# The adapter's first three effective matrices, made during the seventh pair of routed experts

## The reference

```python
# third layer, for each expert e
h = jax.nn.gelu(context_c @ ew1[e] + eb1[e], approximate=True)
y = h @ ew2[e] + eb2[e]
out = out + w_be[:, e][:, None, None] * mask[e][None, :, None] * y
...
# fourth layer: a1, b1, a2, b2 are (B, D, 8), made from the conditioning alone
u = jnp.einsum('btd,bdr->btr', x, a2)
mid = jnp.einsum('btd,dl->btl', x, base_down) + jnp.einsum('btr,blr->btl', u, b2)
mid = jax.nn.gelu(mid, approximate=False)
v = jnp.einsum('blr,btl->btr', b1, mid)
out = jnp.einsum('btl,kl->btk', mid, base_up) + jnp.einsum('bkr,btr->btk', a1, v)
return x + out
```

## Time and profile before

| | us |
|---|---|
| median of 3 runs | 1182.06 (1181.74 to 1182.39) |
| the profiled execution's own time | 1186.63 |
| its span, first to last instruction | 1184.8 |
| PE busy | 1136.6 |
| DVE busy | 766.9 |
| ACT busy | 608.0 |
| POOL busy | 364.4 |
| mean granted PE clock | 0.960 |

### The profile page before, as it was taken

The page is one execution under the profiler, slowest core; times in us unless marked ns, Lnnn a source line. Parts: engine busy times, 40 slices in busy tenths (PEclk is TensorE's granted clock), DMA queues, the critical chain, the costliest instruction groups (busy, mean ns, idle before and its releaser), DMA issues. The chain is left out here.

```text
span 1184.8 us, 58156 instructions
## 1 busy us (share of the span) xinstructions
PE 1136.6 (96%) x23706; PEld 1014.0 (86%) x23706; DVE 766.9 (65%) x2954; ACT 608.0 (51%) x2147; POOL 364.4 (31%) x1372
## 2 busy tenths in 40 slices
PE   5899999999999999999999999899999999999898
PEld 4788888888889888999999998678888888888687
DVE  6566666666666666565565657687666666666697
ACT  4456566566566565555565554533333333333476
POOL 3654344344434344444444440063000000000121
PEclk7759999989989999999999999899999999999899
DMA  8211202202102011110000000000000000000022
GB/s 243 74 44 39 79 4 80 79 4 79 53 31 79 29 54 26 14 15 12 5 4 4 5 4 4 3 1 2 2 2 2 2 1 2 2 2 2 5 75 86
DMA packets 44432, 37.14 MB, mean 31 GB/s; under 512 B 24280, under 2 KB 39946, under 8 KB 44172
## 3 DMA queue, kind: packets, MB, share of 16 engines
q1 hardware_dynamic: 43564, 33.12, 9.2%
q10 hardware_dynamic: 608, 0.30, 0.1%
HBM read 28.42 MB, written 4.98 MB: 28 GB/s over the span
## 5 line engine op out<-in xcount | busy, mean ns | idle before, releaser
L1268 PEld LDWEIGHTS bank<-LH,seq 128*128 128x128 f16 x8192 | 248.8, 96 | 54.0 <-DVE LH L842 46.5
L1268 PE MATMUL bank<-LH,seq 128*128 128x16 f16 x8192 | 283.1, 170 | 12.3 <-DVE LH L842 10.3
L568 ACT ACTIVATE gel<-bank,seq 128x256 f32<-128x256 f32 x256 | 121.5, 475 | 215.0 <-PE bank L1173 211.3
L1171 PE MATMUL bank<-XHL,WE 128*128 128x256 f16 x768 | 210.6, 274 | 5.7 <-issue 2.9
L1171 PE MATMUL bank<-GH,WE 128*128 128x256 f16 x768 | 210.6, 274 | 2.2 <-DVE GH L815 1.8
L1172 PE MATMUL bank<-XHL,WE 128*128 128x256 f16 x768 | 210.7, 274 | 0.0
L1173 PE MATMUL bank<-XHL,WE 128*128 128x256 f16 x768 | 210.7, 274 | 0.0
L1172 PE MATMUL bank<-GH,WE 128*128 128x256 f16 x768 | 210.7, 274 | 0.0
L1173 PE MATMUL bank<-GH,WE 128*128 128x256 f16 x768 | 210.6, 274 | 0.0
L1274 PE MATMUL bank<-LH,seq 128*128 128x16 f16 x4096 | 177.2, 169 | 2.3 <-issue 2.3
L399 POOL TENSOR_TENSOR RH<-rf,RH 128x32 f16<-128x32 f32 x256 | 64.6, 252 | 355.9 <-ACT RH L525 355.9
(11 more groups left out here) (193 smaller groups left out, 2539.6 us busy)
## 6 DMA issues: line engine op xcount, KB each, us to landing
stage<-in_L_cond_ew SPq DMA_DIRECT2D x8, 1024.0 KB, 8.6
stage<-in_L_cond_W SPq DMA_DIRECT2D x8, 1024.0 KB, 5.4
XHL<-in_x SPq DMA_DIRECT2D x8, 512.0 KB, 9.0
out<-WE SPq DMA_DIRECT2D x16, 256.0 KB, 2.1
stage<-in_L_cond_sw SPq DMA_DIRECT2D x2, 1024.0 KB, 5.5
scratch<-rows SPq DMA_DIRECT2D x96, 8.0 KB, 2.3
stage<-in_L_cond_Wx SPq DMA_DIRECT2D x1, 1024.0 KB, 9.1
stage<-in_L_cond_Wh SPq DMA_DIRECT2D x1, 1024.0 KB, 11.3
```

The costliest lines, as they stand in the source:

```text
L568: nc.scalar.activation(gel[:, m % 2, :], banks[m % len(banks)][:, 0:256], ACT.Gelu_apprx_tanh, scale=scale, bias=bias).then_inc(s["a_g"], 1)
L1171: MM(out_, w(HI), x(HI), start=start, stop=False, skip_group_check=True)
L1268: MM(z, LW[:, h, 1, c, tile * P:(tile + 1) * P], LH[:, old, HI, c], start=False, stop=False, skip_group_check=True)
```

## The change

The three matrices (0, 0), (0, 1) and (1, 0) are made during the seventh pair (i = `EARLY_PAIR` = 6). PE calls `matrix` ahead of the slots n = 4, 12 and 20. DVE calls `add_eff` after the split of tile n = 8, 16 and 24 and `weff_lo` after that of n = 14, 22 and 30 (`early_matrix`). ACT calls `weff_hi` after the gelu of n = 12, 20 and 28. For this the three get a home in `seq`, the buffer in which the recurrent layers' weights stood, behind X3; the fourth home of `weff` stays in `WE`. The float32 sum of all three goes through `early_f`, the unused last quarter of a staging buffer. The calls ahead of step 0 fall away. Step 1 on PE gets a wait for the last routed sums (`v_x3`), because mid(1) writes the banks 6 and 7.

```diff
-        weff = adead[:, 0:4096].rearrange("p (s q h c n) -> p s q h c n", s=2, q=2, h=2, c=C)
+        beside = 2 * place[0] + 4096
+        assert beside + 3072 <= 12288
+        weff_home = {(0, 0): seq[:, beside:beside + 1024], (1, 0): seq[:, beside + 1024:beside + 2048],
+                     (0, 1): seq[:, beside + 2048:beside + 3072], (1, 1): adead[:, 0:1024]}
+        weff = {at: home.rearrange("p (h c n) -> p h c n", h=2, c=C) for at, home in weff_home.items()}
+        early_f = dead[:, 3 * C * D:4 * C * D].rearrange("p (c n) -> p c n", c=C)
+        EARLY = ((0, 0), (0, 1), (1, 0))
+        EARLY_PAIR = B // 2 - 2
...
# ACT, in routed_pair after the gelu of slot n
+                    if i == EARLY_PAIR and n in (12, 20, 28):
+                        e = EARLY[n // 8 - 1]
+                        weff_hi(*e, e[1], True)
...
# ACT, ahead of adapter_steps
-            for n, b in ((0, 0), (0, 1), (1, 0)):
-                weff_hi(n, b, b, True)
...
# DVE
+            def early_matrix(n):
+                k, stage_ = divmod(n - 8, 8)
+                if stage_ == 0:
+                    dve.wait_ge(s["v_ad"], 2)
+                    if k:
+                        dve.wait_ge(s["v_w0"], k)
+                    add_eff(*EARLY[k], EARLY[k][1], True)
+                elif stage_ == 6:
+                    weff_lo(*EARLY[k], EARLY[k][1])
...
# DVE, in routed_pair after routed_split(i, n)
+                    if i == EARLY_PAIR and 8 <= n < 32:
+                        early_matrix(n)
...
# DVE, ahead of adapter_steps
-            for n, b in ((0, 0), (0, 1), (1, 0)):
-                add_eff(n, b, b, True)
-            for n, b in ((0, 0), (0, 1), (1, 0)):
-                weff_lo(n, b, b)
...
# PE, in routed_pair ahead of the products of slot n
+                    if i == EARLY_PAIR and n % 8 == 4 and n < 24:
+                        if n == 20:
+                            pe.wait_ge(s["v_ad"], 1)
+                        matrix(*EARLY[n // 8], EARLY[n // 8][1], n != 12)
...
# PE, in step
+                    if b == 1:
+                        pe.wait_ge(s["v_x3"], 6 + 6 * B)
...
# PE, ahead of adapter_steps
-            matrix(0, 0, 0, True)
-            matrix(0, 1, 1, False)
-            matrix(1, 0, 0, True)
```

More of the change, by code:

```diff
@@ L644, in x3_hi, with weff_hi @@
                                      ACT.Copy).then_inc(s["a_x3"], 1)
+            def weff_hi(n, b, slot, first):
+                act.wait_ge(s[f"v_e{n}"], b + 1)
+                if not first:
+                    act.wait_ge(s[("pe_mid", "pe_out")[n]], b * 2 - 2)
+                src = early_f if (n, b) in EARLY else weff_f[:, slot, n]
+                nc.scalar.activation(weff[slot, n][:, HI], src, ACT.Copy).then_inc(s[f"a_e{n}"], 1)
             def routed_pair(i):
@@ L660, in _ @@
             nc.scalar.preload_act_table_set(GELU_SET)
[L662 to L667, removed]
             def step(b, r, prev, this, next1, next2):
@@ L1092, in routed_out, with add_eff, weff_lo @@
                     wslot[:, k, seg, bass.ds(b, 1)], x, ALU.mult, ALU.add).then_inc(s["v_x3"], 1)
+            def add_eff(n, b, slot, first):
+                dve.wait_ge(s[f"pe_e{n}"], b + 1)
+                if not first:
+                    dve.wait_ge(s[f"v_w{n}"], b - 1)
+                V.tensor_tensor(early_f if (n, b) in EARLY else weff_f[:, slot, n],
+                                bank[4 + n][:, :].rearrange("p (c n) -> p c n", c=C),
+                                (down, upT)[n], ALU.add).then_inc(s[f"v_e{n}"], 1)
+            def weff_lo(n, b, slot):
+                dve.wait_ge(s[f"a_e{n}"], b + 1)
+                src = early_f if (n, b) in EARLY else weff_f[:, slot, n]
+                V.tensor_tensor(weff[slot, n][:, LO], src, weff[slot, n][:, HI], ALU.subtract
+                                ).then_inc(s[f"v_w{n}"], 1)
+            def early_matrix(n):
[7 more added lines that the diff above has]
+                    weff_lo(*EARLY[k], EARLY[k][1])
             def routed_pair(i, last):
@@ L1122, in _ @@
                 routed_out(B - 1, 1, seg)
[L1123 to L1137, removed]
             def step(b, r, prev, this, next1, next2):
@@ L1500, in routed_pair @@
                             job(batches[p_], j, experts[t // M])
[L1502 to L1507, removed]
             def matrix(n, b, slot, first):
@@ L1520, in matrix @@
                 last.then_inc(s[f"pe_e{n}"], 1)
+            first = expert_of(0, 0)
+            for j in range(2):
+                routed_hidden(0, j, first)
+            for i in range(B // 2 - 1):
+                routed_pair(i, False)
+            routed_pair(B // 2 - 1, True)
             def step(b, r, prev, this, next1, next2):
@@ L1526, in step @@
                     pe.wait_ge(s["v_w0"], b + 1)
-                    if not isinstance(b, int) or b >= 2:
+                    if b == 1:
+                        pe.wait_ge(s["v_x3"], 6 + 6 * B)
+                    if b >= 2:
                         pe.wait_ge(s["a_mid"], b * 2 - 2)
@@ L1531, in step @@
                             last = three(mid_bank[slot][m][:, 0:256],
-                                         lambda h: weff[:, slot, 0, h, c, m * P:(m + 1) * P],
+                                         lambda h: weff[slot, 0][:, h, c, m * P:(m + 1) * P],
                                          lambda h: X3[:, r, h, c, :], c == 0, c == C - 1)
@@ L1553, in step @@
                             last = three(bank[2 + tt][:, 0:256], lambda h: MH[:, 1 - slot, h, l, tt * P:(tt + 1) * P],
-                                         lambda h: weff[:, 1 - slot, 1, h, l, :], False, l == C - 1)
+                                         lambda h: weff[1 - slot, 1][:, h, l, :], False, l == C - 1)
                         last.then_inc(s["pe_out"], 1)
-            matrix(0, 0, 0, True)
-            matrix(0, 1, 1, False)
-            matrix(1, 0, 0, True)
             adapter_steps(pe, step)
```

## The result

The changed kernel takes **1175.76 us** in the median of 6 runs (1174.18 to 1180.68), the kernel before 1182.22 in 6 runs beside it. The ratio is 0.9946 with a 95% interval of 0.9925 to 0.9967, so the change saves 6.4 us (3.9 to 8.9). The forecast was 1174.3, with a range of 1172.8 to 1178.5.

A forecast was written before the change was run, and what follows sets the result against it. PE, busy 96% of the span, was taken as the bound. Seam 4.48 plus low clock 5.29 made 9.77; less 0.73 stalls and 1.26 matrices, 7.8 us off 1182.06 gave 1174.3, range 1172.8 to 1178.5.

The forecast's parts named there:

- The seam of 4.48 us: Between the last routed matmul and the adapter's first product PE waits; closing this was to gain 4.48 us.
- The low clock costs 5.29 us: From mid(0) to mid(4), the adapter's first steps: 18.37 us traced against 13.08 at full clock, 5.29 to be had.
- The gain sits in both: The 7.8 us gain was taken off both the profiled execution (1186.63) and the median (1182.06), giving 1174.3.
- The three matrices cost 1.26: In the seventh pair, three early matrices at 0.42 us each on PE, a loss of 1.26, bounds 0.66 and 1.8.
- The collision in step 0 and the stall of 0.73: POOL's x3 part holds up DVE's low parts in adapter step 0 by 0.95 us; PE then waits 0.73 us.
- The margin of 0.13 us: In later adapter steps POOL comes 0.13 us after DVE's second low part is issued, so DVE goes first.
- The collision repeats: Rival: DVE needs 4.42 us per adapter step, PE loses 8.5 us, time 1182.8; chance 0.10 in full, 0.10 in part.
- The clock stays low anyway: Rival: the gain stops at PE's 0.7 us wait around step 2; price 5.29, time 1179.6, chance 0.06.
- the matrices each cost a whole slot: Rival, seventh pair: three matrices at 1.31 us each, 3.9 in place of 1.26, time 1177.0, chance 0.05.
- the costly pair: Rival in which the seventh pair's three matrices take 3.9 us in place of 1.26: 1177.0, chance 0.05.
- the partial collisions: Rival: DVE and POOL collide in successive adapter steps but this breaks off on the way; time between, chance 0.10.
- the clock rival: Rival: the clock stays low in the adapter despite the closed seam; time 1179.6, chance 0.06, partly counted as faster.

The follow-up runs named there:

- warm: The kernel before, with 30 unused matmuls on PE during the waits of the seam: 1180.42 us, ratio to before 0.9980.
- after_again: The changed kernel run once more without edit: 1176.46 us, ratio to the kernel before 0.9952.
- price: The changed kernel with twelve spare product pairs of 128 rows in the third pair and twelve of 24 rows in the fifth: these grew by 2.63 and 5.11 us.
- collide: The changed kernel with ACT's order changed so that POOL comes during DVE's first low part: 1185.74 us, ratio to before 1.0037.

## Why the prediction was right, and where its size was off

The direction, the mechanism and the range were right. The forecast of 1174.3 lies 1.5 us below the measured 1175.76. That the measured time also lies within the forecast's own 1173.0 to 1175.8 is in part luck, since neither end allows for what moved it, the two lengths of the low clock.

- **The seam of 4.48 us closed.** Right: one slot lies between the last routed matmul and mid(0).
- **The low clock costs 5.29 us. This is the term that was mis-sized.** It was read from one execution, as the difference to full clock. The mechanism holds (warm: filler in the seam, clock 1.00). But the kernel before has two sorts of executions. From mid(0) to mid(4) they take 18.37 and 18.84 us, or 15.06, 15.15 and 14.93. Against the same 13.08 that is a loss of 5.29 and 5.76 in the one sort, and of 1.98, 2.07 and 1.85 in the other, of which 0.6 is the stall behind the collision with POOL that the changed kernel has too. The stretch of the changed kernel is accordingly 7.8 and 8.3 us below the one sort, and 4.4 below the other (402.1 to 397.7). A mixture of two and three of these gives 5.8; the measurements gave 6.4 (3.9 to 8.9) and, by the ratio of after_again, 5.7 (3.5 to 7.8). Five traces don't fix the mixture. The step that let this in is "The gain sits in both": the traced execution took 4.57 us more than the median, and its 7.8 was taken off a median whose runs no trace shows to be of its sort. (The two traced long executions took 1186.63 and 1187.33 us, the three short ones 1180.69 to 1181.56.) Warm gives 4.6 against the first trace, which is about the 5.29 less the stall of 0.61 that appears at full clock.
- **The three matrices cost 1.26.** Measured 1.28 in the seventh pair; the changeover of 0.10 each way came out at 0.43 a matrix in price. DVE, ACT and SP hid their part, as forecast: PE is busy for all of the 43.20 us.
- **The collision in step 0 and the stall of 0.73.** The collision came where it was put: DVE's low parts at 1115.35 and 1115.95, which are the forecast's 1116.80 and 1117.40 less the 1.44 by which the last routed matmul came earlier in this trace. From mid(0) to mid(4) the trace has 13.69 against an undisturbed 13.08, a stall of 0.61. The last link was another than forecast: the chain ends in ACT's output copy of batch 0 (0.38 at 1119.03), for which the identity products wait, and not in DVE's MH. (MH's low part ended less than 0.1 us before out(1) began, so the two links lie close together.) That copy stood on ACT behind the matrix's copy, which waited for the late addition.
- **The margin of 0.13 us.** Right: POOL came 2.40 after DVE's second addition, as worked out, and no further collision followed; steps of 3.71 from there.
- **The rivals.** "The collision repeats" did not occur in the changed kernel, but collide shows it is real: 4.42 a step, as computed, and enough to end above before. The forecast had put 1182.8 on it, which took the optimistic 7.8 as its base; with the measured 6.4 it comes to 1184.2, and 1185.74 was measured. "The clock stays low anyway" and "the matrices each cost a whole slot" are excluded by the trace of after. The chances were added up wrongly: with the forecast at 0.65, the costly pair 0.05, half the partial collisions 0.05 and the clock rival at most 0.06, "faster" comes to 0.81 at most, not 0.85, and "same" to 0.15 or more, not 0.11.

## What to carry to other kernels

Before a gain is read from a stretch at low clock, profile several executions: here the same wait of 4.5 us was followed by 3.4 or by 13.65 us of half clock, and one profile would have given either. Where the next engine is only 6% faster than the bound (3.47 to 3.71 us a step), work out at which moment a GpSimd instruction becomes ready against the vector engine's two-input instructions. A reordering on a third engine that moved this by about half a microsecond (POOL from 2.40 to 1.9 us behind DVE's second addition) turned a gain of 0.5% into a loss of 0.4%. Small products of few rows are cheaper next to each other than spread out, since each change of rows costs 0.1 us on the tensor engine.

## What the runs showed of the hardware beyond that

Low clock after a seam came in two lengths, 3.4 us (three traces) and 13.65 (two), with PE busy without a gap from mid(0) until the clock rose in both. DVE's loss to POOL repeats exactly, 0.95 us in each of twelve steps: a waiting POOL instruction went ahead between two DVE instructions whose recorded times overlap, even where the second DVE instruction followed the first without a pause.
